# Attention on one core: TensorE's order laid over two key steps, every second values product cut into two halves of 256 queries

## Chip, cores and metric

One core of a Trainium2 chip (trn2) runs the kernel. The metric is the time of one execution on the device in microseconds (us); lower is better. Engines are named as in the profile: PE is TensorE (PEld its weight loads), DVE is VectorE, ACT is ScalarE, POOL is GpSimd and SP is SyncE, which issues the DMAs.

## What is computed

A transformer block with adaptive layer norm, on 2 sequences of 2048 tokens of 256 features, 16 heads of 16, all in 32-bit floats. Shortened:

```python
h = layernorm(x) * (1 + ca) + sa
q, k, v = split(h @ W_qkv.T + b_qkv)            # 16 heads of 16
logits = einsum('bhqd,bhkd->bhqk', q, k) / 4
logits = where(causal, logits, -inf)
o = einsum('bhqk,bhkd->bhqd', softmax(logits), v)
x = x + ga * (o @ W_out.T + b_out)
h = layernorm(x) * (1 + cb) + sb
x = x + gb * ffn(h)     # two linear maps, each with a routed low-rank part, relu between
```

The change touches only the attention in the middle.

## The kernel before

Three stages run one after the other: projections (to about 140 us of the profiled execution), attention (about 140 to 1005 us), output projection and feed-forward (to the end). Only the attention matters here.

**Tiling.** Heads go in 8 groups `g` of 4 (`GH`), queries in blocks `J` of 512. A pair (g, J) is a *unit*, 32 in all (line 39), with J running 0, 1, 2, 3 in one group and 3, 2, 1, 0 in the next. A unit has 4(J+1) *steps*, one for each 128 keys, so 4, 8, 12 or 16; all units together have 320 (`STEPS`, line 42). The last four steps of a unit lie on the causal diagonal: they skip 0, 128, 256 and 384 queries (`skip_of`) and add a mask. A unit's first step is always even and its last odd.

**A step n, by engine.** PE makes four logits tiles (line 811), one per head h: keys on the 128 partitions, up to 512 queries in the free dimension, into one of three PSUM banks (`L_BUFS` = 3, index 4n+h modulo 3). Even heads stand on rows 0 to 63 of the array, odd heads on rows 64 to 127. ACT takes the exponential of each tile into `prob` (line 1011). A logits tile must wait until the exponential three tiles earlier has freed its bank (line 809). Two steps later (`PV_LAG`) PE multiplies the values: `values(n - 2)` (line 829), four heads side by side in the array's column strips, 128 x 32 each, accumulated over the unit's steps in the one bank `O_BANK`. The weights `vw` hold values and ones, so the softmax denominator comes out too. `vw` and `prob` are plain 32-bit floats, and each product is recorded as two matmuls. At a unit's end ACT copies the bank out (`copy_out`, line 1002), and the next unit's first values wait for that (`o_out`, line 827).

**Fills.** The row maxima that the exponential needs are found one or more units ahead: PE makes queries-by-keys tiles, a *fill* (line 791), into two bank pairs (`S_BANK`), DVE reduces each (lines 1157 and 1161), and a fill waits until the fill two before it has been reduced (line 776). One fill is two matmuls of up to 512 columns, one on each half of the array's rows, and 4 or 8 mask matmuls more on the diagonal (line 767). Once per unit a *turn* fill (line 779) transposes the finished maxima, DVE copies them to `mT` (line 1186) and SP spreads them by four DMAs (line 470) into rows of the query stack; a unit's first logits wait for these (`m_in`, line 807).

**Order of the work.** PE's order is written out at lines 840 to 850. Which fills go into which step is planned by `slots()` (line 120): `ORDER[1 + n]` is the list for step n. There are 608 fills for 320 steps, 212 steps have two, 62 one, 29 three. Taken for each two steps (n even, n + 1), 86 of the 160 pairs have 4 fills, 24 have 2, 21 have 5, 16 have 3, the rest other numbers; of units 3 to 29, 19 pairs have 5 and 16 have 3. Units 30 and 31 have 3 fills in all.

**What the change and the steps of the prediction touch.** `mask` (762), `fill` (773), `logits` (800), `values` (820), PE's loop (840), and ACT's place for `copy_out` (1013).

Of the kernel before, what the change touches and what calls it, by code (L numbers as in the profile page):

```python
# [5 lines left out]
P = 128  # L6
# [17 lines left out]
BLK = 512  # L24
# [132 lines left out]
def until(eng, sem, count):  # L157
    if count > 0:
        eng.wait_ge(sem, count)


def build_program(nc, x, cT, wmod, wqkvT, bqkv, bv, woutT, bout, w1, b1, ar1, bl1, w2, b2, ar2, bl2, out):
# [4 lines left out]
    with ExitStack() as whole:  # L167
# [239 lines left out]
        with nc.Block() as block:  # L407
# [290 lines left out]
            def _(pe):  # L698
# [60 lines left out]
                    project(n)  # L759


                def mask(banks, col, table):

                    for half in range(2):
                        for par in range(2):
                            rows = slice(par * STACK, (par + 1) * STACK)
                            last = pe.matmul(ps[:, banks[par], col:col + P], eye_h[rows, half, :],  # L767
                                             table[rows, half, :], start=False, stop=True, skip_group_check=True)
                            if half == 1 and table is mask_kh:
                                last.then_inc(st_done, 1)  # L770
                    return last

                def fill(e):
                    ev = EVENTS[FILLS[e]]
                    bank = S_BANK + 2 * (e % 2)
                    until(pe, max_red, e - 1)
                    if ev[0] == "turn":
                        pe.wait_ge(m_low, ev[1] + 1)
                        pe.transpose(ps[:, bank, 0:P], mparts[:].bitcast(F32),
                                     ident[:]).then_inc(fill_done, 1)  # L780
                        return
                    _, u, r, pairs, cb, width, on_diagonal = ev
                    g, J = UNITS[u]
                    q, k = qst[g % 2], kst[g % 2]
                    if e == 0 or EVENTS[FILLS[e - 1]][0] == "turn" or EVENTS[FILLS[e - 1]][1] != u:
                        for j in range(J + 1):
                            pe.wait_ge(kq_in[g % 2][j], 16 * K_DMAS * (g // 2 + 1))
                    for at, p in enumerate(pairs):
                        for par in range(2):
                            rows = slice(par * STACK, par * STACK + ROWS)  # L790
                            last = pe.matmul(ps[:, bank + par, at * width:(at + 1) * width],  # L791
                                             q[rows, p, J * BLK + r * P:J * BLK + (r + 1) * P],
                                             k[rows, p, cb * BLK:cb * BLK + width],
                                             start=(at == 0), stop=True, skip_group_check=(at > 0))
                    if on_diagonal:
                        for at in range(len(pairs)):
                            last = mask((bank, bank + 1), (at + 1) * width - P, mask_qh)
                    last.then_inc(fill_done, 1)

                def logits(n, pair):  # L800

                    u, t = STEPS[n]
                    g, J = UNITS[u]
                    skip = skip_of(n)
                    banks = [L_BANK + (4 * n + 2 * pair + par) % L_BUFS for par in range(2)]
                    if n == FIRST[u] and pair == 0:
                        pe.wait_ge(m_in[u % 2], 16 * M_DMAS * (u // 2 + 1))
                    for par in range(2):
                        until(pe, exp_done, 4 * n + 2 * pair + par - L_BUFS + 1)
                        rows = slice(par * STACK, par * STACK + ROWS + MROWS)  # L810
                        last = pe.matmul(ps[:, banks[par], 0:BLK - skip],  # L811
                                         kst[g % 2][rows, pair, t * P:(t + 1) * P],
                                         qst[g % 2][rows, pair, J * BLK + skip:(J + 1) * BLK],
                                         start=True, stop=True)
                        if not diagonal(n):
                            last.then_inc(st_done, 1)
                    if diagonal(n):
                        mask(banks, 0, mask_kh)

                def values(n):  # L820
                    u, t = STEPS[n]
                    g, J = UNITS[u]
                    skip = skip_of(n)
                    pe.wait_ge(exp_done, 4 * (n + 1))
                    if n == FIRST[u]:
                        pe.wait_ge(v_wide, g + 1)
                        until(pe, o_out, u)
                    for h in range(GH):
                        last = pe.matmul(ps[32 * h:32 * h + 32, O_BANK, skip:BLK], vw[:, g % 2, t, h, :],  # L829
                                         prob[:, n % P_BUFS, h, 0:BLK - skip],  # L830
                                         start=(t == 0), stop=(n == LAST[u]), tile_position=(0, 32 * h))
                    last.then_inc(pv_done, 1)

                pe.wait_ge(h_out, NBLK * 2 * KC)
                pe.wait_ge(v_out, NBLK)
# [117 lines left out]
            def _(act):  # L953
# [45 lines left out]
                def copy_out(u):  # L999
                    act.wait_ge(pv_done, LAST[u] + 1)  # L1000
                    until(act, o_stored[u % 2], 16 * O_DMAS * (u // 2))
                    act.copy(o_sb[:, u % 2, :], ps[:, O_BANK, :]).then_inc(o_out, 1)  # L1002

                first_stage_over(act)
                for n in range(NS):
                    width = BLK - skip_of(n)
                    until(act, pv_done, n - P_BUFS + 1)
                    for h in range(GH):
                        i = 4 * n + h
                        act.wait_ge(st_done, i + 1)  # L1010
# [347 lines left out]
```

## Time and profile before

| | us |
|---|---|
| median of 3 runs | 1361.06 |
| lowest and highest of them | 1353.09, 1361.54 |
| the profiled execution, its own time | 1362.05 |
| its span, first to last instruction | 1360.2 |
| attention, first exponential to last step's | 139 to 1005 |
| granted TensorE clock, mean over the span | 0.948 of full |
| busy over the span: PE, DVE, ACT, POOL | 90%, 70%, 59%, 13% |

A busy share of PE is the time in which at least one matmul is recorded; the ends of matmuls are modelled, so the starts are the safer reading. An engine's idle time stands with what ended it.

### The profile page before, as it was taken

To read this page: it belongs to the slowest core of one execution; us is meant where nothing else is said; L and a number is where in the kernel's file an instruction comes from. 1 tells how busy PE (TensorE), PEld (TensorE's weight loads), DVE (VectorE), ACT (ScalarE), POOL (GpSimd) and SP (SyncE) were. 2 spreads that over 40 slices of the span, in tenths; PEclk is the share of its full clock that TensorE was granted. 3 is DMA by queue.
4 is the path that set the end of the run, shared out by engine and by line. 5 is a ranking of instruction groups with operands and counts; after the bars stand their busy time and mean duration, and the time that the engine had idled before them with its cause. 6 is when DMAs were issued, how large, how long until landed. Compare 5 with 4: busy or idle time off the path is not lost.

```text
span 1360.2 us, 23639 instructions
## 1 busy us (share of the span) xinstructions
PE 1221.2 (90%) x9456; PEld 714.0 (52%) x9456; DVE 950.9 (70%) x1247; ACT 804.3 (59%) x1616; POOL 175.7 (13%) x125
## 2 busy tenths in 40 slices
PE   2988889999999999999999999999962999999997
PEld 2875433444444444444444444434322888888886
DVE  7767897888787887787887777865203567666654
ACT  2542366777677777677777667777631544444442
POOL 8003700000111000000000000000003132323211
PEclk9987799999999999999999999999865999999999
DMA  4684130031041021031021021000013011111200
GB/s 154 217 267 175 40 72 10 8 84 35 31 115 47 10 77 37 10 89 40 9 62 52 10 79 49 9 9 11 9 34 123 1 62 49 42 43 55 63 16 32
DMA packets 58118, 79.53 MB, mean 58 GB/s; under 512 B 12680, under 2 KB 28752, under 8 KB 58008
## 3 DMA queue, kind: packets, MB, share of 16 engines
q1 hardware_dynamic: 58008, 78.01, 18.9%
q8 instruction: 75, 1.23, 0.4%
q14 instruction: 35, 0.29, 0.1%
HBM read 47.57 MB, written 29.62 MB: 57 GB/s over the span
## 4 chain that ended last, share of the span: by engine, by line
PE 66%; DVE 16%; ACT 8%; issue 7%; DMA 1%; POOL 1%; SPq 0%; POOLq 0%; ACTq 0%; DVEq 0%
PE ps L829 20%; PE ps L811 17%; PE ps L373 8%; PE ps L791 8%; ACT prob L1011 6%; PE ps L767 5%; PE ps L905 5%; DVE mx L1161 4%; DVE hid_lo L1273 4%; DVE xhat L401 2%; DVE stats L391 1%; ACT o_sb L1002 1%; DVE x L1227 1%; DVE x L1223 1%; DMA rd<-rden_rows 1%
## 5 line engine op out<-in xcount | busy, mean ns | idle before, releaser
L1011 ACT ACTIVATE prob<-ps 128x512 f32<-128x512 f32 (+3 forms) x1280 | 597.7, 535 | 258.1 <-PE ps L767 136.3
L1161 DVE TENSOR_REDUCE mx<-ps 128x2 f32<-128x1024 f32 (+1 forms) x512 | 593.2, 1190 | 171.7 <-PE ps L791 97.6
L811 PE MATMUL ps<-qst,kst 64*128 64x512 f32 (+3 forms) x1280 | 380.9, 448 | 13.1 <-ACT prob L1011 7.3
L811 PEld LDWEIGHTS ps<-qst,kst 64*128 64x128 f32 x1280 | 174.7, 186 | 323.7 <-ACT prob L1011 283.7
L829 PE MATMUL ps<-prob,vw 128*32 128x512 f32 (+3 forms) x2560 | 306.6, 551 | 9.8 <-ACT o_sb L1002 9.8
L791 PE MATMUL ps<-kst,qst 62*128 62x512 f32 (+3 forms) x1280 | 247.7, 417 | 20.9 <-DVE mx L1161 17.7
L791 PEld LDWEIGHTS ps<-kst,qst 62*128 62x128 f32 x1280 | 125.9, 191 | 64.0 <-DVE mx L1161 55.7
L767 PE MATMUL ps<-mask_kh,eye_h 64*128 64x128 bf16 x1024 | 100.6, 225 | 0.0
L829 PEld LDWEIGHTS ps<-prob,vw 128*32 128x32 f32 x2560 | 51.7, 108 | 74.6 <-ACT prob L1011 49.7
L1273 DVE TENSOR_TENSOR hid_lo<-hidf,hid_hi 128x512 fp32r<-128x512 f32 x64 | 73.1, 1182 | 12.8 <-ACT hid_hi L1055 12.7
L905 PE MATMUL ps<-w_hi,hid_hi 128*128 128x284 f32 x256 | 78.6, 328 | 2.0 <-ACT hid_hi L1055 2.0
L905 PE MATMUL ps<-w_lo,hid_hi 128*128 128x284 f32 x256 | 76.8, 321 | 0.0
L1157 DVE TENSOR_REDUCE mx<-ps 128x4 f32<-128x512 f32 x64 | 59.7, 954 | 21.6 <-PE ps L767 21.5
L1055 ACT ACTIVATE hidf<-ps,b_sb 128x512 f32<-128x512 f32 x64 | 44.0, 688 | 47.5 <-PE ps L894 47.5
L614 POOL COPY vw<-v_nat 128x1024 f32<-128x1024 f32 x8 | 8.3, 1040 | 469.0 <-PE ps L829 468.8
L767 PE MATMUL ps<-mask_qh,eye_h 64*128 64x128 bf16 x1024 | 66.6, 224 | 0.0
L373 PE MATMUL ps<-hT_hi,w_hi 128*128 128x512 f32 x128 | 53.2, 415 | 9.0 <-ACT hid_hi L1055 9.0
L905 PEld LDWEIGHTS ps<-w_hi,hid_hi 128*128 128x128 f32 x256 | 54.8, 214 | 4.0 <-ACT hid_hi L1055 3.6
L1038 ACT ACTIVATE gexp<-gexp 128x12 f32<-128x12 f32 x16 | 3.4, 212 | 89.4 <-DVE gexp L1243 89.4
L905 PEld LDWEIGHTS ps<-w_lo,hid_hi 128*128 128x128 f32 x256 | 55.0, 215 | 0.4
L667 POOL TENSOR_TENSOR o_raw<-o_raw,rd 128x1024 f32<-128x1024 f32 x8 | 19.5, 2440 | 254.2 <-DMA rd<-rden_rows 254.2
L767 PEld LDWEIGHTS ps<-mask_kh,eye_h 64*128 64x128 bf16 x1024 | 42.9, 97 | 17.1 <-issue 7.2
(150 smaller groups left out, 1402.8 us busy)
## 6 DMA issues: line engine op xcount, KB each, us to landing
qk_parts<-parts SPq DMA_DIRECT2D x32, 512.0 KB, 4.2
qst<-qk_parts SPq DMA_DIRECT2D x192, 64.0 KB, 2.3
kst<-qk_parts SPq DMA_DIRECT2D x192, 64.0 KB, 2.3
xs<-in_x SPq DMA_DIRECT2D x16, 512.0 KB, 7.2
o_all<-o_sb SPq DMA_DIRECT2D x32, 256.0 KB
o_raw<-o_all SPq DMA_DIRECT2D x16, 256.0 KB
rd<-rden_rows SPq DMA_DIRECT2D x16, 256.0 KB
out<-y SPq DMA_DIRECT2D x8, 512.0 KB, 3.1
```

The costliest lines, as they stand in the source:

```text
L373: last = pe.matmul(out, lhs(i, k), rhs(j, k), start=(start and k == 0 and n == 0), stop=(stop and k == chunks - 1 and n == len(PASSES) - 1))
L401: last = dve.tensor_scalar(xhat[:, t, :], xs[:, t, :], mv[:, t, 0:1], rstd[:, t:t + 1], ALU.subtract, ALU.mult)
L767: last = pe.matmul(ps[:, banks[par], col:col + P], eye_h[rows, half, :], table[rows, half, :], start=False, stop=True, skip_group_check=True)
L791: last = pe.matmul(ps[:, bank + par, at * width:(at + 1) * width], q[rows, p, J * BLK + r * P:J * BLK + (r + 1) * P], k[rows, p, cb * BLK: ...
L811: last = pe.matmul(ps[:, banks[par], 0:BLK - skip], kst[g % 2][rows, pair, t * P:(t + 1) * P], qst[g % 2][rows, pair, J * BLK + skip:(J + ...
L829: last = pe.matmul(ps[32 * h:32 * h + 32, O_BANK, skip:BLK], vw[:, g % 2, t, h, :], prob[:, n % P_BUFS, h, 0:BLK - skip], start=(t == 0), ...
L905: last = pe.matmul(ps[:, Y_BANK + t, 0:D + ZP], hid[u][:, m, t * P:(t + 1) * P], w2_p[v][:, m, :], start=(e == 0), stop=(e == len(order) - 1))
L1011: act.activation(prob[:, n % P_BUFS, h, 0:width], ps[:, L_BANK + i % L_BUFS, 0:width], ACT.Exp).then_inc(exp_done, 1)
L1055: act.activation(dst, ps[:, H_BANK + m % 2, :], ACT.Relu, bias=b1_sb[:, m:m + 1]).then_inc(f1_out, 1)
L1157: dve.tensor_reduce(mx[:, u % 2, :, :, r, cb], ps[:, bank:bank + 2, 0:2 * width].rearrange("p a (h x) -> p a h x", h=2), AX, ALU.max).then ...
L1161: dve.tensor_reduce(mx[:, u % 2, :, pairs[0], r, cb], ps[:, bank:bank + 2, 0:width], AX, ALU.max).then_inc(max_red, 1)
L1273: dve.tensor_tensor(hid[1][:, m, :], hidf[:, m % HRING, :], hid[0][:, m, :].bitcast(F32), ALU.subtract).then_inc(hid_lo_done, 1)
```

## The change

PE's order is laid over two steps, n even and n + 1. The logits of single heads, or of pairs that are not of the same step, alternate with fills and with the values of step n - 2, cut into two halves of the queries; the values of step n - 1 stay whole. `logits` takes a list of heads. The key mask is added right behind each such list, for its heads. The first three fills of the two steps have fixed places, all the others go to the end. ACT's copy of a finished unit comes one step later than before, less one head. Lags, buffers, the planner and all other engines' orders stay. Core of the diff:

```diff
-                def logits(n, pair):
+                def logits(*heads):
+                    for n, h in heads:
...
+                        until(pe, exp_done, 4 * n + h - L_BUFS + 1)
...
+                    if diagonal(heads[0][0]):
+                        mask_keys(heads)
...
-                def values(n):
+                def values(n, part=None):
...
+                    lo, hi = 0, BLK - skip
+                    if part == 0:
+                        hi = hi // 2
+                    if part == 1:
+                        lo = hi // 2
                     pe.wait_ge(exp_done, 4 * (n + 1))
-                    if n == FIRST[u]:
+                    if n == FIRST[u] and part != 1:
                         pe.wait_ge(v_wide, g + 1)
                         until(pe, o_out, u)
...
-                for n in range(NS):
+                for n in range(0, NS, 2):
+                    es = [*ORDER[1 + n], *ORDER[2 + n]]
+                    logits((n, 0), (n, 1))
+                    for e in es[0:1]:
+                        fill(e)
+                    logits((n, 2))
                     if n >= PV_LAG:
-                        values(n - PV_LAG)
-                    logits(n, 0)
-                    for e in ORDER[1 + n][:2]:
+                        values(n - 2, 0)
+                    logits((n, 3), (n + 1, 0))
+                    for e in es[1:2]:
                         fill(e)
-                    logits(n, 1)
-                    for e in ORDER[1 + n][2:]:
+                    if n >= PV_LAG:
+                        values(n - 2, 1)
+                    logits((n + 1, 1))
+                    for e in es[2:3]:
                         fill(e)
-                for n in range(NS - PV_LAG, NS):
-                    values(n)
+                    logits((n + 1, 2), (n + 1, 3))
+                    if n >= PV_LAG:
+                        values(n - 1)
+                    for e in es[3:]:
+                        fill(e)
+                values(NS - 2)
+                values(NS - 1)
...
-                        if h == 1 and n - PV_LAG in UNIT_AT_END:
-                            copy_out(UNIT_AT_END[n - PV_LAG])
+                        if h == 0 and n - PV_LAG - 1 in UNIT_AT_END:
+                            copy_out(UNIT_AT_END[n - PV_LAG - 1])
```

`mask_keys(heads)` adds, for each half of the key mask, one matmul per head of the list, and raises `st_done` with the second.

## Rows read from the trace of the kernel before

**Rows 1.** The page: busy time, share, instructions; the clock in 40 slices.

```profile
PE 1221.2 (90%) x9456; PEld 714.0 (52%) x9456; DVE 950.9 (70%) x1247; ACT 804.3 (59%) x1616; POOL 175.7 (13%) x125
...
PEclk9987799999999999999999999999865999999999
```

**Rows 2.** Busy time by window (us; instructions; clock, DMA share, GB/s), one unit each.

```profile
645.70:687.70 42.00, 41.09 (x325) 17.03 (x321) 34.87 (x35) 31.52 (x66) 0.00 (x0) 1.00 0.02 8
594.00:614.38 20.38, 19.50 (x160) 8.30 (x156) 16.81 (x16) 14.83 (x34) 0.00 (x0) 1.00 0.36 98
614.38:645.70 31.32, 29.88 (x257) 13.00 (x253) 23.09 (x25) 23.25 (x50) 0.00 (x0) 1.00 0.14 40
584.16:594.00 9.84, 9.38 (x97) 4.96 (x93) 7.88 (x11) 6.51 (x18) 1.04 (x1) 1.00 0.27 88
...
971.15:1006.00 34.85, 31.29 (x211) 11.80 (x203) 3.27 (x6) 20.94 (x48) 0.00 (x0) 0.76 0.05 17
```

**Rows 3.** Timeline of one step: start, duration, engine, line [idle before <- releaser].

```profile
599.68 0.50 PE L811 MATMUL ps<-qst,kst 64*128 64x512 f32 x2
600.02 0.40 PE L791 MATMUL ps<-kst,qst 62*128 62x512 f32 x2
600.25 0.40 PE L791 MATMUL ps<-kst,qst 62*128 62x512 f32 x2
600.27 2.07 ACT L1011 ACTIVATE prob<-ps 128x512 f32<-128x512 f32 x4 [0.74 <-PE ps L811]
600.48 0.40 PE L811 MATMUL ps<-qst,kst 64*128 64x512 f32 x1
600.92 0.18 PEld L811 LDWEIGHTS ps<-qst,kst 64*128 64x128 f32 x1 [0.48 <-ACT prob L1011]
601.35 1.07 PE L829 MATMUL ps<-prob,vw 128*32 128x512 f32 x8
602.35 0.50 PE L811 MATMUL ps<-qst,kst 64*128 64x512 f32 x2
602.94 2.07 ACT L1011 ACTIVATE prob<-ps 128x512 f32<-128x512 f32 x4 [0.60 <-PE ps L811]
```

**Rows 4.** Waits, 227 to 950 us: who for whom, total, times, longest.

```profile
PEld ps L811 <- ACT prob L1011: 249.3, 396, 0.9
...
PEld ps L791 <- DVE mx L1161: 29.3, 75, 0.8
```

**Rows 5.** Groups by form, 300 to 900 us: count, busy us, mean ns, idle before.

```profile
L1161 DVE TENSOR_REDUCE mx<-ps 128x2 f32<-128x1024 f32 x319 | 380.2, 1221 | 91.5 <-PE ps L791 68.1 <-PE ps L767 20.1
L1011 ACT ACTIVATE prob<-ps 128x512 f32<-128x512 f32 x630 | 331.1, 601 | 101.9 <-PE ps L811 78.9 <-PE ps L767 22.0
```

**Rows 6.** Chain of work on the diagonal: start us, us, what.

```profile
678.56 0.13 PE ps L767 x4
...
682.70 0.33 PE ps L767 x3
...
685.51 0.78 PE ps L829 x8
...
687.55 0.57 PE ps L829 x8
```

**Rows 7.** Timeline where a unit begins.

```profile
647.73 0.42 PE L829 MATMUL ps<-prob,vw 128*32 128x128 f32 x8
648.08 0.69 PE L811 MATMUL ps<-qst,kst 64*128 64x512 f32 x2
...
649.65 0.59 ACT L1002 COPY o_sb<-ps 128x512 f32<-128x512 f32 x1
...
650.39 1.06 PE L829 MATMUL ps<-prob,vw 128*32 128x512 f32 x8 [0.41 <-ACT o_sb L1002]
```

**Rows 8.** Timeline of a unit's maxima on SP.

```profile
220.74 2.60 SPq L470 DMA_DIRECT2D qst<-mT  x4
```

**Rows 9.** Timeline where the clock is low.

```profile
768.16 1.93 PE L829 MATMUL ps<-prob,vw 128*32 128x512 f32 x8
...
770.02 0.29 PEld L811 LDWEIGHTS ps<-qst,kst 64*128 64x128 f32 x2 [1.66 <-issue]
```

More of the change, by code:

```diff
@@ L759, in _, with mask_queries @@
                     project(n)
-                def mask(banks, col, table):
+                def mask_queries(bank, col):
                     for half in range(2):
@@ L766, in mask, with mask_keys @@
                             rows = slice(par * STACK, (par + 1) * STACK)
-                            last = pe.matmul(ps[:, banks[par], col:col + P], eye_h[rows, half, :],
-                                             table[rows, half, :], start=False, stop=True, skip_group_check=True)
-                            if half == 1 and table is mask_kh:
+                            last = pe.matmul(ps[:, bank + par, col:col + P], eye_h[rows, half, :],
+                                             mask_qh[rows, half, :], start=False, stop=True, skip_group_check=True)
+                    return last
+                def mask_keys(heads):
+                    for half in range(2):
+                        for n, h in heads:
+                            rows = slice(h % 2 * STACK, (h % 2 + 1) * STACK)
+                            last = pe.matmul(ps[:, L_BANK + (4 * n + h) % L_BUFS, 0:P], eye_h[rows, half, :],
+                                             mask_kh[rows, half, :], start=False, stop=True, skip_group_check=True)
+                            if half == 1:
                                 last.then_inc(st_done, 1)
-                    return last
                 def fill(e):
@@ L796, in fill @@
                         for at in range(len(pairs)):
-                            last = mask((bank, bank + 1), (at + 1) * width - P, mask_qh)
+                            last = mask_queries(bank, (at + 1) * width - P)
                     last.then_inc(fill_done, 1)
-                def logits(n, pair):
+                def logits(*heads):
+                    for n, h in heads:
+                        u, t = STEPS[n]
+                        g, J = UNITS[u]
+                        skip = skip_of(n)
+                        if n == FIRST[u] and h == 0:
+                            pe.wait_ge(m_in[u % 2], 16 * M_DMAS * (u // 2 + 1))
+                        until(pe, exp_done, 4 * n + h - L_BUFS + 1)
+                        rows = slice(h % 2 * STACK, h % 2 * STACK + ROWS + MROWS)
+                        last = pe.matmul(ps[:, L_BANK + (4 * n + h) % L_BUFS, 0:BLK - skip],
+                                         kst[g % 2][rows, h // 2, t * P:(t + 1) * P],
+                                         qst[g % 2][rows, h // 2, J * BLK + skip:(J + 1) * BLK],
+                                         start=True, stop=True)
+                        if not diagonal(n):
+                            last.then_inc(st_done, 1)
+                    if diagonal(heads[0][0]):
+                        mask_keys(heads)
+                def values(n, part=None):
                     u, t = STEPS[n]
@@ L804, in logits @@
                     skip = skip_of(n)
[L805 to L818, printed above, removed]
-                def values(n):
-                    u, t = STEPS[n]
-                    g, J = UNITS[u]
-                    skip = skip_of(n)
+                    lo, hi = 0, BLK - skip
[3 more added lines that the diff above has]
+                        lo = hi // 2
                     pe.wait_ge(exp_done, 4 * (n + 1))
-                    if n == FIRST[u]:
+                    if n == FIRST[u] and part != 1:
                         pe.wait_ge(v_wide, g + 1)
@@ L828, in values @@
                     for h in range(GH):
[L829 to L832, printed above, removed]
+                        last = pe.matmul(ps[32 * h:32 * h + 32, O_BANK, skip + lo:skip + hi], vw[:, g % 2, t, h, :],
+                                         prob[:, n % P_BUFS, h, lo:hi],
+                                         start=(t == 0 and part != 1), stop=(n == LAST[u] and part != 0),
+                                         tile_position=(0, 32 * h), skip_group_check=True)
+                    if part != 0:
+                        last.then_inc(pv_done, 1)
                 pe.wait_ge(h_out, NBLK * 2 * KC)
```

## Prediction

> **What bounds the kernel now.** I read the page first: PE is recorded busy for 90% of the span, DVE for 70% and ACT for 59% [rows 1]. That looks like a PE-bound kernel, in which an order can bring nothing. The windows by unit say the same (41.09 of 42.00 us on PE, 34.87 on DVE, 31.52 on ACT [rows 2]), but a recorded matmul includes its latency, so I went to the starts in the timeline of one step [rows 3].
>
> The step is a loop with a fixed length. Call the four logits tiles L0 to L3 and their exponentials E0 to E3. L0 and L1 start at 599.68; E0 starts at 600.27, 0.59 later; L3 needs the bank that E0 frees and its weights load at 600.92, 0.65 later; the values start at 601.35 (0.43) and the next L0 at 602.35 (1.00). Sum 0.59 + 0.65 + 0.43 + 1.00 = 2.67 us, and nearly all full steps of units 3 to 29 take that, with one fill or two. ACT works 2.07 of it and idles 0.60. So neither engine is full: the wait of L3 for E0 sets the pace. The table of waits confirms it: PE's loads of logits weights waited 249.3 us for the exponential, 396 times, against 29.3 us for DVE [rows 4].
>
> From the same rows come PE's true costs. The first slot behind a values visit takes 0.34 (599.68 to 600.02, its weight load in the open), each further slot 0.23 (600.02, 600.25, 600.48). A slot is up to two matmuls, one per half of the rows. A single tile loaded in the open and followed by values takes 0.43, so with its weights already loaded about 0.43 - 0.11 = 0.32. A values visit of 512 columns takes 1.00. With two fills PE's own work in a step is 0.34 + 0.23 + 0.23 + 0.32 + 1.00 = 2.12; the other 0.55 is the wait.
>
> **The change, a full pair of steps with 4 fills.** Before: 2 x 2.67 = 5.34. After, with F0 to F3 the fills, t = 0 at F3, which follows the whole values, and L0 to L7 the eight tiles:
> - F3 0, L0 and L1 0.34, F0 0.57, L2 0.80, half values at 1.12. For a half I take the visit of 256 columns, 0.57 [rows 6]; two halves cost 1.14 against 1.00.
> - L3 at 1.69. L4 needs E1. E0 starts 0.49 behind L0's loaded start (0.40 of matmul and 0.09 to ACT), at 0.83; exponentials follow each other by (2.07 - 0.60) / 3 = 0.49 [rows 3, 5], so E1 starts at 1.32 and ends at 1.92, L4 loads at 1.97: a wait of 0.28. F1 at 2.31 (0.11 load, 0.23), half values at 2.63, to 3.20.
> - L5 with F2's even half 0.34, F2's odd half with L6 0.23, L7 0.32, whole values at 4.09, next F3 at 5.09. E2 (1.81), E3 (2.30) and E4 (2.79, done 3.4) are in time for L5, L6 and L7.
>
> So 5.09, of which 4.81 is PE's work (0.57 more than before) and 0.28 a wait (1.10 before). Gain 0.25 per full pair. ACT needs 8 x 0.49 = 3.9. DVE starts reductions every 1.14 us (two in 2.36, one takes 1.22 [rows 5]), so four need 4.56: covered, but close. Without F3 the pair takes 0.34 less, since before the loop hid that fill for nothing.
>
> **The other pairs.**
> - Unit's first pair: its values are narrow (256 columns in two halves at 0.35 each, then 128, 0.35 from 647.73 to 648.08 [rows 7]). With the same timetable and no F3 left from the pair before: about 4.0.
> - Second pair: the copy of the finished unit now stands behind E0, so it starts at 0.83 + 0.49 = 1.32, takes 0.59, and the values start some 0.14 behind it (650.39 against 650.24 [rows 7]), at 2.05 instead of 1.12. L4's wait is swallowed; period about 5.7.
> - Diagonal pairs: masks cost 0.13 behind a pair and up to 0.33 at the end of a group [rows 6]; five groups now, four before, and single heads no longer share a slot with a fill. Adding up gives 10.1 for the last two pairs against about 10.0. No gain there.
>
> Units of 16 steps: 4.0 + 5.7 + 4 x 5.09 + 10.1 = 40.2 against 42.00; of 12: 4.0 + 5.7 + 10.2 + 10.1 = 30.0 against 31.32 (I take -1.4); of 8: 19.8 against 20.38; of 4: about 9.7 against 9.84 [rows 2]. Units 3 to 29 are 8, 7, 6 and 6 of these: 8 x 1.8 + 7 x 1.4 + 6 x 0.6 + 6 x 0.15 = 28.7 us.
>
> **Where it gives back.** 19 pairs there have 5 fills, and two of them now stand together at the end. The next pair's F0 needs the first one's bank: matmul 0.49, reduction 1.22, hand-overs 0.09 make 1.80, while PE is there after 0.34 + 0.23 + 0.23 = 0.80. That holds PE for 1.0 us, less the 0.28 of L4, plus a slot of 0.23: 0.95. What is queued behind F0 is L2, and behind it the values. Before, three fills in a step cost some 0.3 themselves. Net +0.6 each, +11.4. The 16 pairs with 3 fills save 0.34 each, -5.4.
>
> Turn fills of units 1 to 3 move to the end of the next to last pair, two steps before the logits that wait for them instead of three or more. Their four DMAs take 2.60 us to issue [rows 8] and land later still; the last pair covers some 4.3. I take +2 in all (0 to 6). The units before 3 carry three fills a step and are paced by DVE: no change. Units 30 and 31 run partly at clock 0.76 [rows 2] and have few fills: -1 (+4 to -6, as the clock falls).
>
> Cut values raise PE's instructions, not the wait counts of other engines; `prob` has four buffers, and ACT never comes near that wait. POOL's and SP's later work for a unit moves by one step and has several steps of room.
>
> **Sum.** -28.7 + 11.4 - 5.4 + 2 - 1 = -21.7. The profiled execution took 1362.05, 1.0 above the median; 1362.05 - 21.7 = 1340.3, so I say 1340.
>
> **A rule weighed.** The rows show that going from logits to values and back costs 0.14 more than the streaming of a 256-column visit's two passes (0.57 against 0.43) plus 0.11 for a load in the open. The Trainium skill, TensorEngine Tiling (Array Packing), Key Properties, says that changing the tiling mode, not just the tile, drains TensorE; logits are row tiles and values column tiles, so the new order has six such changes in two steps instead of four. By that rule alone the change would cost and not save; the trace agrees that each has a price, and that price is in the 4.81 above.
>
> **Rivals.**
> - *The switches eat the gain.* If a half costs 0.70 rather than 0.57, or single tiles don't share slots with the fills next to them (up to three slots of 0.23 where I counted them shared), a full pair is at 5.3 to 5.4 and nothing is left: 1356 to 1366, say 1361. For it: no lone tile next to a fill is in the rows with both weights loaded. Against: the 0.57 is measured on the same instruction form. Chance 0.20.
> - *More falls away.* L4 waits less (E0 follows a loaded pair by 0.43 if ACT's hand-over is short), and the end fills don't hold PE, because DVE has its slack when they come. -28.7 - 5.4 and another 100 x 0.06: about 1322. Chance 0.18.
> - *The clock falls (slower).* At half clock a whole values visit takes 1.86 (768.16 to 770.02 [rows 9]) instead of 1.00. Place: the first two pairs of a unit, where streams are narrow and PE now waits 0.9 us for the copy. Before, it happened once in units 3 to 29 (the visit of rows 9) and again at the end. It decides from 11 such falls on; one in each of 31 units adds about 60 and gives 1400, half as many 1370. Against: elsewhere PE idles less than before. Chance 0.12, typical time 1380.
>
> **How the numbers follow.** Forecast 0.50, rivals 0.20, 0.18, 0.12. The forecast's own spread is 1330 to 1351. A difference under 1% (13.6 us) is what a measurement here can't tell from none. Faster by over 1% (below 1347.5): 0.44 of the forecast's 0.50 and the 0.18, 0.62. Slower by over 1% (above 1374.7): 0.11, most of the clock rival. The rest, 0.27, is same. Range 1318 to 1362: low from the second rival with its bounds, high from the middle of the first; 0.2 stays outside, the clock rival and the edges of the others.
>
> **What would show it.** Right: full pairs start every 5.1 us; the longest wait on PE is L4's, 0.3 us once in two steps, so logits waiting for exponentials fall from 249 us to under 80; ACT's busy share rises slightly; line 829's visits number 480 for 320 steps; values behind a copy wait about 0.9 us. The DVE waits of the fills rise above 29 us. Wrong: full pairs at 5.3, halves above 0.6, lone tiles that start only after the fill beside them, or more slices of the clock under 9 between 230 and 950 us.

## The result: slightly slower, and the profile after

| | before | after |
|---|---|---|
| median, us | 1360.21 (4 runs, 1353.09 to 1361.54) | 1372.59 (4 runs, 1364.18 to 1377.42) |
| ratio, 95% interval | | 1.0084 (1.0048 to 1.012) |
| the profiled execution, span | 1360.2 | 1368.1 |

The kernel became 0.8% slower. That is inside the 1% I called "same", with its interval (0.5 to 1.2%) wholly on the slow side; I had forecast 1340 us and a range up to 1362.

The page of the kernel after first: busy time and the clock by slices. Beside [rows 1], PE has 1272 matmuls and 11 us of busy time more, DVE 6 and ACT 4 us; the shares are the same.

```profile
PE 1232.6 (90%) x10728; PEld 747.3 (55%) x10728; DVE 956.7 (70%) x1247; ACT 808.5 (59%) x1616; POOL 175.6 (13%) x125
...
PEclk9998599999999999999999999999985899999998
```

Where the time went shows when the attention is cut just ahead of unit 3 and unit 28, at the start of the last exponential of the unit before. The last window ends at the last exponential of the step before the last; the first begins with the load of ACT's table at 139.2, which the rows before counted as the first exponential (that one starts at 140.5). Columns after the window: its length, busy us (instructions) of PE, PEld, DVE, ACT and POOL, granted clock, DMA share, GB/s. After:

```profile
139.20:234.34 95.14, 82.71 (x689) 39.71 (x691) 76.92 (x79) 46.10 (x98) 22.23 (x14) 0.80 0.15 40
234.34:919.69 685.35, 660.68 (x6747) 318.41 (x6743) 535.96 (x567) 492.91 (x1050) 24.15 (x38) 1.00 0.15 43
919.69:1014.84 95.15, 92.70 (x936) 43.59 (x932) 41.89 (x48) 74.92 (x162) 0.00 (x0) 1.00 0.03 11
827.75:847.53 19.78, 19.38 (x192) 8.81 (x188) 17.40 (x16) 14.88 (x34) 0.00 (x0) 1.00 0.37 98
664.12:706.64 42.52, 41.31 (x389) 18.82 (x385) 34.79 (x34) 31.58 (x67) 0.00 (x0) 1.00 0.02 8
```

The same cuts before:

```profile
139.24:227.20 87.96, 74.45 (x609) 34.64 (x611) 75.12 (x79) 45.73 (x99) 22.32 (x14) 0.90 0.18 44
227.20:898.13 670.93, 649.65 (x5723) 290.60 (x5719) 532.97 (x568) 488.51 (x1050) 24.18 (x38) 1.00 0.15 44
898.13:1004.62 106.49, 98.19 (x773) 40.60 (x769) 41.66 (x49) 75.18 (x161) 0.00 (x0) 0.93 0.03 12
```

So +7.2 us in units 0 to 2, +14.4 in units 3 to 27, -11.3 in units 28 to 31, and -2.3 behind the attention. Unit 25 (8 steps, the fourth window) takes 19.78 against 20.38 for a unit of its kind, unit 19 (16 steps) 42.52 against 42.00 [rows 2].

**The plain pair came out as worked out.** The timeline of PE in the third pair of unit 11, four fills and none on the diagonal:

```profile
459.54 0.50 PE L799 MATMUL ps<-kst,qst 62*128 62x512 f32 x2
459.88 0.39 PE L818 MATMUL ps<-qst,kst 64*128 64x512 f32 x2
460.12 0.39 PE L799 MATMUL ps<-kst,qst 62*128 62x512 f32 x2
460.35 0.39 PE L818 MATMUL ps<-qst,kst 64*128 64x512 f32 x1
460.66 0.64 PE L843 MATMUL ps<-prob,vw 128*32 128x256 f32 x8
461.23 0.78 PE L818 MATMUL ps<-qst,kst 64*128 64x512 f32 x2
461.57 0.67 PE L799 MATMUL ps<-kst,qst 62*128 62x512 f32 x2
462.18 0.64 PE L843 MATMUL ps<-prob,vw 128*32 128x256 f32 x8
462.75 0.49 PE L818 MATMUL ps<-qst,kst 64*128 64x512 f32 x1
462.75 0.72 PE L799 MATMUL ps<-kst,qst 62*128 62x512 f32 x2
463.08 0.62 PE L818 MATMUL ps<-qst,kst 64*128 64x512 f32 x2
463.63 1.06 PE L843 MATMUL ps<-prob,vw 128*32 128x512 f32 x8
464.62 0.51 PE L799 MATMUL ps<-kst,qst 62*128 62x512 f32 x2
```

From the first start, half values come 1.12 later, L3 at 1.69, half values at 2.64, L5 beside the fill's even half at 3.21, whole values at 4.09, the next F3 at 5.08. The prediction had 1.12, 1.69, 2.63, 3.20, 4.09, 5.09. L4's wait is the 0.78 of two matmuls at 461.23.

**What the other pairs do.** Because the load of the table was counted as an exponential, every boundary of a pair, here and in the experiments, is one exponential early: a pair's time runs from the last exponential before it to its own last one. Sums over units hardly change by that, but the split between neighbouring pairs does. The last column has the split between true first exponentials. After - before in us, in all, units 3 to 27:

```
kind of pair                                 pairs   as counted   first exponentials
follows a pair with five or more fills          19      +18.8          +18.3
has five or more fills, follows none such       16       -8.0           -3.3
of the rest: has fills on the diagonal          40      +10.3          +12.9
of the rest: no fill on the diagonal            53       -6.8          -13.5
```

### The profile page after: what moved, and what is told of

It reads as the page before. It is cut to its first block, busy times and chain, and to the rows that moved or that the text cites. A ratio compares the mean times of both kernels' runs of the same rounds, so it can differ in the third digit from the quotient of the medians.

```text
span 1368.1 us, 26183 instructions
## 1 busy us (share of the span) xinstructions
PE 1232.6 (90%) x10728; PEld 747.3 (55%) x10728; DVE 956.7 (70%) x1247; ACT 808.5 (59%) x1616; POOL 175.6 (13%) x125
## 4 chain that ended last, share of the span: by engine, by line
PE 72%; DVE 18%; ACT 4%; issue 3%; DMA 1%; SPq 0%; POOL 0%; DVEq 0%; ACTq 0%; POOLq 0%
PE ps L843 21%; PE ps L818 18%; PE ps L799 10%; PE ps L373 9%; PE ps L933 7%; DVE mx L1189 5%; DVE hid_lo L1301 4%; PE ps L776 3%; DVE xhat L401 2%; PE ps L767 2%; ACT prob L1039 2%; ACT o_sb L1030 1%; DVE stats L391 1%; DVE x L1255 1%; DVE x L1251 1%
## 5 line engine op out<-in xcount | busy, mean ns | idle before, releaser
L818 PE MATMUL ps<-qst,kst 64*128 64x512 f32 (+3 forms) x1280 | 389.8, 434 | 0.6 <-ACT prob L1039 0.4
L843 PE MATMUL ps<-prob,vw 128*32 128x256 f32 (+1 forms) x3832 | 340.5, 428 | 12.7 <-ACT o_sb L1030 12.5
L799 PE MATMUL ps<-kst,qst 62*128 62x512 f32 (+3 forms) x1280 | 320.7, 433 | 28.6 <-DVE mx L1189 25.7
L818 PEld LDWEIGHTS ps<-qst,kst 64*128 64x128 f32 x1280 | 186.0, 188 | 177.8 <-ACT prob L1039 138.0
L799 PEld LDWEIGHTS ps<-kst,qst 62*128 62x128 f32 x1280 | 147.4, 192 | 124.9 <-DVE mx L1189 60.7
L843 PEld LDWEIGHTS ps<-prob,vw 128*32 128x32 f32 x3832 | 77.2, 109 | 126.9 <-issue 61.9
L776 PE MATMUL ps<-mask_kh,eye_h 64*128 64x128 bf16 x1024 | 106.5, 225 | 0.0
L767 PE MATMUL ps<-mask_qh,eye_h 64*128 64x128 bf16 x1024 | 79.3, 225 | 0.0
L373 PE MATMUL ps<-hT_hi,w_lo 128*128 128x512 f32 x128 | 50.9, 398 | 0.0
```

The costliest lines, as they stand in the source:

```text
L373: last = pe.matmul(out, lhs(i, k), rhs(j, k), start=(start and k == 0 and n == 0), stop=(stop and k == chunks - 1 and n == len(PASSES) - 1))
L767: last = pe.matmul(ps[:, bank + par, col:col + P], eye_h[rows, half, :], mask_qh[rows, half, :], start=False, stop=True, skip_group_check= ...
L776: last = pe.matmul(ps[:, L_BANK + (4 * n + h) % L_BUFS, 0:P], eye_h[rows, half, :], mask_kh[rows, half, :], start=False, stop=True, skip_g ...
L818: last = pe.matmul(ps[:, L_BANK + (4 * n + h) % L_BUFS, 0:BLK - skip], kst[g % 2][rows, h // 2, t * P:(t + 1) * P], qst[g % 2][rows, h // ...
L843: last = pe.matmul(ps[32 * h:32 * h + 32, O_BANK, skip + lo:skip + hi], vw[:, g % 2, t, h, :], prob[:, n % P_BUFS, h, lo:hi], start=(t == ...
```

## Experiments

All times below are medians with the kernel before of the same chips beside them, and ratios to it. The kernel after was not timed again with them; its ratio is 1.0084.

### Where the fifth fill stands

**e1_spread.** The kernel after, with a pair's fills dealt out differently.

```diff
-                    for e in es[3:]:
+                    for e in at[3]:      # at = places(es): one maxima fill per place,
                         fill(e)          # a turn fill goes in front of the next one
```

> Kernel after, with the fifth fill of a pair of steps moved: a turn fill goes in front of the fill that follows it and takes no place of its own, so each of the four places has one maxima fill (lists of more than four maxima fills are divided as evenly as they go). No fill stands behind another one at the end of a pair. Theory, the held bank: in the kernel after, a pair that follows one with five fills is about 1.0 to 1.4 us longer (5.77 us for the last pair of a unit of 16 steps against 4.49 us where the pair before had four), since the first of two fills at the end has not been reduced when the next pair's first fill wants its bank. Then these pairs fall to 4.5 us (last of a unit) and some 0.9 us each are won, 19 times: -14 to -20 us in units 3 to 27, and some us in units 0 to 2, which would put it at 1343 to 1358, with the kernel after at about 1370 and before at 1360. Rival, these pairs are long by their own masks and narrow tiles: they stay at 5.7 us and the time stays within 4 us of the kernel after.

Measured 1369.87 against 1360.1, ratio 1.0058 (1.0022 to 1.0094): 0.3 points under the kernel after, with intervals that overlap, so no gain to speak of. Pair by pair, both sides of the expectation hold. The last pair of unit 11 falls from 5.78 to 4.48 us, as the held bank says, and the pair with the turn rises from 5.49 to 6.52. The reason is one line of its trace: the fill behind the turn now finds the bank of the fill before the turn unreduced.

```profile
477.49 0.51 PE L799 MATMUL ps<-kst,qst 62*128 62x512 f32 x2 [0.71 <-DVE mx L1197]
```

A turn uses a bank pair like any fill. Put next to another fill anywhere, it makes two in a row; the hold only moved one pair ahead. Part of the rest is the clock, which was at half for 24 us of units 3 to 31 here (10 in the profiled execution after).

**e10_fourth_fill_before_values.** The kernel after, with two of the fills moved apart.

```diff
+                    end = 4 if len(es) >= 5 else 3
+                    for e in es[3:end]:
+                        fill(e)
                     if n >= PV_LAG:
                         values(n - 1)
-                    for e in es[3:]:
+                    for e in es[end:]:
```

> Kernel after; in pairs with five or more fills the fourth stands before the whole values instead of behind them, so the last two are a values visit (1.00 us) apart. Theory, the held bank: the first of the two is reduced 1 us earlier, the next pair's first fill waits 0.2 us instead of 1.0, and the pair after one with a turn and four fills falls from 5.77 us (last pair of a unit) to 4.7 to 4.9, while the pair with five fills stays at 5.5 to 5.7. 19 times 0.6 to 0.9 us: -11 to -17 us against the kernel after, 1353 to 1361. Rival, DVE has no slack in these pairs and the time only moves, as it did where the turn shared the first place (5.5 to 6.5 us there, 5.77 to 4.48 behind it): within 5 us of the kernel after.

Measured 1358.0 against 1359.96, ratio 0.9988 (0.9966 to 1.001), so 1.0% or 13 us less than the kernel after. The hold in the kernel after, in the last pair of unit 11 (486.54 is the first of the two fills at the end, 487.09 its reduction, and the next pair's first fill stands until that is over):

```profile
484.00 2.58 DVE L1189 TENSOR_REDUCE mx<-ps 128x2 f32<-128x1024 f32 x2 [1.16 <-PE ps L799]
...
486.54 0.74 PE L799 MATMUL ps<-kst,qst 62*128 62x512 f32 x4
...
487.09 2.36 DVE L1189 TENSOR_REDUCE mx<-ps 128x2 f32<-128x1024 f32 x2 [0.51 <-PE ps L799]
...
488.37 0.19 PEld L799 LDWEIGHTS ps<-kst,qst 62*128 62x128 f32 x2 [1.01 <-DVE mx L1189]
```

DVE had been idle for 1.16 and 0.51 us shortly before: it had the time, not the data. In e10 the same place reads:

```profile
477.60 1.07 PE L843 MATMUL ps<-prob,vw 128*32 128x512 f32 x8
478.59 0.49 PE L799 MATMUL ps<-kst,qst 62*128 62x512 f32 x2
...
479.53 0.50 PE L799 MATMUL ps<-kst,qst 62*128 62x512 f32 x2 [0.19 <-DVE mx L1192]
```

The last pair is 5.17 instead of 5.78, the one with five fills unchanged at 5.49. In the traces, units 3 to 27 take 10 us less than in the kernel after and units 0 to 2, where the edit acts too, 3 us less. Of all that the new order costs this is the largest part that one edit took away.

### Masked fills: work that the old wait covered

**e2_after_mask_work_twice, e3_before_mask_work_twice.** Both kernels, with the query mask's matmuls of each diagonal fill issued again with a table of zeros.

```diff
+                            for half in range(2):
+                                for par in range(2):
+                                    ...
+                                    last = pe.matmul(ps[:, bank + par, col:col + P], eye_h[rows, half, :],
+                                                     none_h[rows, half, :], start=False, stop=True, ...)
```

> Kernel after, with the query mask's matmuls of every diagonal fill issued a second time against a table of zeros (same result; 512 more places of two 128-column matmuls side by side, 400 of them in units 3 to 27). It doubles the work whose price in the new order I had left out. Theory, exposed PE work: without the long wait for the exponential nothing covers it, so each place costs its 0.06 us except where a pair still waits: +20 to +30 us against the kernel after. Rival, pairs with diagonal fills are slow in the kernel after for another reason (the reductions, or the bank pairs): under +10 us.

> Kernel before, with the same doubled query mask matmuls. Theory: in the old order a step's third logits wait 0.45 us for the first exponential behind the fills, so the doubled work fits into that wait for the most part: +2 to +10 us against the kernel before, and at least 12 us less than the same edit costs in the kernel after. Rival, it is no matter of cover: both orders pay the same, 20 us or more.

Measured: after with doubled masks 1398.8, ratio 1.0249 (1.0189 to 1.0309), so +1.65 points or 22 us over the kernel after, as expected. Before with doubled masks 1377.31, ratio 1.0113 (1.0083 to 1.0143), +15 us, more than the 2 to 10 expected, and the gap between the two only 7 us instead of at least 12.

The pairs tell why. Unit 11 has three pairs in a row whose 12 fills include its six on the diagonal, all in the first two pairs (16 places of two mask matmuls side by side); without masks they would take three plain pairs:

```
                                     three pairs, us    beyond plain pairs
before                               16.00              0.0  (3 x 5.34)
before, masks doubled                16.51             +0.5
after                                16.25             +1.0  (3 x 5.09)
after, masks doubled                 17.02             +1.8
```

In the old order the first helping of masks costs nothing and the second half a microsecond: the cover, L3's wait [rows 3, 4], was for the most part used up by the masks that were there. My expectation for e3 took it for free. A step of the kernel before with two diagonal fills, eight mask matmuls, starts its next logits after 2.67 us like one without [rows 3]:

```profile
460.78 0.50 PE L811 MATMUL ps<-qst,kst 64*128 64x512 f32 x2
...
461.35 0.29 PE L767 MATMUL ps<-mask_qh,eye_h 64*128 64x128 bf16 x4
...
461.76 0.29 PE L767 MATMUL ps<-mask_qh,eye_h 64*128 64x128 bf16 x4
...
463.45 0.50 PE L811 MATMUL ps<-qst,kst 64*128 64x512 f32 x2
```

In the new order the first helping costs 0.06 us a place at once. The timeline after, with masks between fill and logits, each of them on PE's path (0.21 us for the four places from 470.30, 0.10 for the two from 471.00):

```profile
469.95 0.50 PE L799 MATMUL ps<-kst,qst 62*128 62x256 f32 x4
470.30 0.40 PE L767 MATMUL ps<-mask_qh,eye_h 64*128 64x128 bf16 x8
470.51 0.48 PE L818 MATMUL ps<-qst,kst 64*128 64x512 f32 x2
470.82 0.33 PE L799 MATMUL ps<-kst,qst 62*128 62x384 f32 x2
471.00 0.29 PE L767 MATMUL ps<-mask_qh,eye_h 64*128 64x128 bf16 x4
471.10 0.48 PE L818 MATMUL ps<-qst,kst 64*128 64x512 f32 x1
```

Other units say the same. Take the pairs with four fills inside a unit, off the diagonal and not behind five fills, between first exponentials: before, all 18 take 5.33 or 5.34 us; after, the seven without masks take 5.08, the eight with 8 places 5.58, and the two with 12 places also 5.58. Units 3 to 27 have 400 such places, so I estimate at most 400 x 0.06 = 24 us for what the prediction left out. The masks were not taken away in a run, only doubled, so the price of the first helping rests on these comparisons of pairs and starts.

### The cut and the change of tiling

**e4_before_cut_in_place.** The kernel before, with every even step's values in two halves that stay together.

```diff
+                    cuts = (0, width // 2, width) if n % 2 == 0 else (0, width)
+                    for c, (lo, hi) in enumerate(zip(cuts, cuts[1:])):
                         for h in range(GH):
```

> Kernel before, with the values of every even step cut into two halves of the queries that stay next to each other. It prices the cut alone, without a change of tiling between the halves. In the old order the values lie on the loop that sets the step. If two halves cost 0.57 each against 1.00 (0.14 more), 160 cuts give +22 us. If the extra of a visit is only its way in and out (the halves follow each other without draining), it is 0.03 each, +4 us. Rival: a cut costs more than I took, 0.3 us, +48 us.

Measured 1361.4 against 1360.1, ratio 1.0003 (0.9976 to 1.0031). A cut whose halves stay together costs nothing that shows. The interval excludes +22 us and reaches +4, so the time alone leaves my lower figure of 0.03 us a cut open; the starts speak against it. A visit with 16 matmuls of 256 columns ends where one with 8 of 512 does, 1.00 us later:

```profile
657.36 1.07 PE L832 MATMUL ps<-prob,vw 128*32 128x256 f32 x16
658.36 0.50 PE L811 MATMUL ps<-qst,kst 64*128 64x512 f32 x2
```

So the 0.14 that two separate halves cost over a whole (0.57 twice against 1.00) is the way in and out, between values and logits. The Trainium skill, TensorEngine Tiling (Array Packing), Key Properties, says that a change of the tiling mode drains TensorE; this run agrees, in that the price follows the change and not the cut.

**e7_whole_values.** The kernel after, with the cut undone.

```diff
-                        values(n - 2, 0)
+                        values(n - 2)
...
-                    if n >= PV_LAG:
-                        values(n - 2, 1)
```

> Kernel after, with the values of the even step whole in the place of their first half. It undoes the cut and nothing else. By my timetable a pair with four fills off the diagonal then takes 5.28 us (PE stands at the sixth and seventh logits for the exponentials of the fourth and fifth), against 5.09 us with halves and 5.34 us in the old order. Two changes of tiling fewer save 0.35 us of PE's work in each pair, so pairs with masked fills, where PE's work decides, get shorter by up to 0.3 us. In all within 8 us of the kernel after. Rival, the switches are what costs the kernel after its gain: then every pair gets shorter and it is 15 us or more faster than the kernel after.

Measured 1373.76, ratio 1.0107 (1.0079 to 1.0135), within 0.3 points of the kernel after. The plain pair takes 5.23 us in its timeline, where 5.28 was worked out:

```profile
459.23 0.50 PE L799 MATMUL ps<-kst,qst 62*128 62x512 f32 x2
...
462.56 0.98 PE L818 MATMUL ps<-qst,kst 64*128 64x512 f32 x2
463.46 1.06 PE L843 MATMUL ps<-prob,vw 128*32 128x512 f32 x8
464.46 0.50 PE L799 MATMUL ps<-kst,qst 62*128 62x512 f32 x2
```

The 0.98 of two matmuls at 462.56 is the wait of L7. The cut is worth 0.15 us a plain pair, and it is not what made the kernel slower. That refutes the rival of the switches, by which every pair had to get shorter. The pairs with masks did not gain their 0.3 us either: the two of unit 11 take 10.86 us together, and 10.78 in the kernel after.

### The two ends of the attention

**e6_old_first_units.** The kernel after, with units 0 to 2 in the old order: `if not NEW[n]:` runs the old loop's body for the two steps, and ACT's copy goes where that needs it.

> Kernel after, with units 0 to 2 in the old order. In the kernel after these units take 95.2 us against 88.0 us, and the clock is at half for 39 us of them against 17 us; the list of the first pair has 14 fills, of which 11 stand in one row at its end, where PE issues a fill each 1.14 us and does nothing else. Theory, the bunch of fills lets the clock stay low and delays the first units: -5 to -8 us against the kernel after. Rival, the clock's stretches there are chance: within 3 us.

Measured 1362.28 against 1361.05, ratio 1.0016 (0.9997 to 1.0035): 9 us less than the kernel after. The first three units take 90.9 us in this trace, and 95.1, 98.4, 92.1 and 90.9 in the traces of the new order that keep the bunch (after, e2, e10, e7), against 88.0, 90.0, 88.9, 88.0 and 90.8 in those of the old (before, e3, e4, e5, e8). In e1, which has the new order but deals these fills out, they take 87.7 us, with 19 us at half clock: one trace, but it points to the bunch and not to the rest of the new order. That the bunch of 11 fills does this by way of the clock is not settled: the half clock in this stretch was 39 us after, 39 in e2, but 25 in e7, and 28 here in the old order. The part it costs is 4 us by the traces and 9 by the medians; the path was not isolated.

**e5_late_only.** The old order up to unit 26, the new one from unit 27 on.

> Old order (kernel before) up to unit 26, new order from the first pair of unit 27 on, with ACT's copy of a unit placed to match. Theory: the new order pays where a pair has at most three fills and few of them on the diagonal, since then PE's work for a pair is short and the wait for the exponential is what goes. The two traces give -1.7 us for unit 27 and -10.4 us for units 28 to 31 (the sum of the pairs' differences), so 1346 to 1352 with before at 1360. Rival: the late part is faster in the kernel after only because its clock happened to be high there (its low stretches between 940 and 1014 us are absent, before has 10 us of them): then no more than -5 us.

Measured 1347.42 against 1361.05, ratio 0.991 (0.9883 to 0.9937). Units 28 to 31 take 92.1 us up to the last pair, in this trace as in that of the kernel after, and 91.1 to 95.6 in the eight others with the new order there; the three traces with the old order (before, e3, e4) have 102.5 to 103.1. In those three the clock fell in unit 30, in the two pairs with one fill each (8.30 and 6.66 us before, instead of 5.5 and 5.7); in no trace of the new order did it fall there, though in two (e2, e10) it was at half for 3.4 us in unit 28. So I estimate that some 4 of the 10 us come from the clock that stays up and 6 from shorter pairs.

**e8_mixed, e9_mixed_turned, e11_turned_old_order.** Each kind of pair in the order that is shorter for it; the same with the old order turned, so that logits come first and values last in each step; the turned old order alone.

```diff
+                        for m in (n, n + 1):
+                            logits((m, 0), (m, 1))
+                            for e in ORDER[1 + m][:2]:
+                                fill(e)
+                            logits((m, 2), (m, 3))
+                            for e in ORDER[1 + m][2:]:
+                                fill(e)
+                            if m >= PV_LAG:
+                                values(m - 2)
```

> Each pair of steps in the order that was shorter for its kind in the two traces: the new order for pairs of units 3 to 27 with at most four fills, none of them on the diagonal (the second pair of a unit also with them), which do not follow a pair with five fills and are not the last of a unit, and for units 28 to 31; the old order for all others. 67 pairs and the last units are in the new order. The sum of the pairs' measured differences is -20 us, if each keeps its time beside neighbours of the other kind: 1340 us with before at 1360. If gains are given back at the seams, or the clock falls more often, half of that: 1350.

Measured 1347.95, ratio 0.9907 (0.9888 to 0.9926). The edit puts 48 pairs of units 3 to 27 and the 20 of the last four units in the new order. Units 3 to 27 gained nothing (672.8 us against 670.9): in unit 12 an old pair behind a new one took 7.02 instead of 5.17 us, and the new one behind it 4.38 instead of a plain 5.09, a loss of 1.1 at that seam.

> The same choice of pairs as in the mixed kernel, but the old order is turned in its circle: a step's two pairs of logits and its fills first, the values of two steps ago last, so that every pair of steps, old or new, begins with logits and ends with values. ACT's copy of a unit has the place of the new order everywhere. Theory, the mixed kernel lost its gain at the seams (whole values, the end fill, and whole values again stand in a row where an old pair follows a new one, 7.02 us for a pair of 5.15 us, and the next new pair gets back 0.7 of it): without them the sum of the pairs' differences comes, -17 to -22 us against before: 1339 to 1344. Rival, new pairs need new neighbours (their gain comes from the phase of the exponentials that the pair before leaves): no better than the mixed kernel, 1348.

Measured 1351.48, ratio 0.9941 (0.9919 to 0.9964): wrong. The seam is smaller, not gone (6.53 and 5.04, where 5.17 and 5.47 stand in the pure kernels): the rival is right that a new pair's gain needs new neighbours.

> All pairs in the turned old order of the kernel just described; the control for it. The circle of logits, fills and values is the same as in the kernel before, entered at another place, so full steps take 2.67 us and the time is that of the kernel before within 4 us, the beginnings of units apart, where the copy of the finished unit comes later. If it were 5 us or more faster, the turn and not the new order would be what helps.

Measured 1349.42 against 1359.96, ratio 0.9933 (0.9907 to 0.9959). I had expected a difference within 4 us. In the traces 7 us of the gain lie in units 3 to 27 and 5 in units 28 to 31. Steps inside a unit are the same (5.34 a pair), but the second pair of unit 11 takes 4.75 instead of 5.49 us, for 0.13 and 0.22 lost in the first and the last; between first exponentials it is the first pair that falls, from 5.33 to 4.35, and 0.15 and 0.42 are lost. A unit's first values no longer wait 0.41 us for the copy [rows 7]: such waits came to 9.8 us in 25 visits between 227 and 1000 us before, and the turned order's trace lists none. PE makes the logits first, and the copy lies beside them. PE's and ACT's timelines there, with no wait in front of the values:

```profile
441.58 0.61 ACT L1044 COPY o_sb<-ps 128x512 f32<-128x512 f32 x1
...
441.95 0.40 PE L821 MATMUL ps<-qst,kst 64*128 64x512 f32 x2
442.33 1.07 PE L846 MATMUL ps<-prob,vw 128*32 128x512 f32 x8
443.32 0.50 PE L821 MATMUL ps<-qst,kst 64*128 64x512 f32 x2
```

**e12_turned_then_new.** The turned old order up to unit 26, the new one from unit 27 on: `NEW = {n: n >= FIRST[27] for n in range(0, NS, 2)}`.

> The turned old order up to unit 26, the new order from unit 27 on. It joins the two parts that were found shorter: the turned order wins some 7 us in units 3 to 26 over the kernel before (the copy of a finished unit no longer holds the values of the next), and units 28 to 31 take 92.1 us in the new order against 97.3 in the turned and 102.5 in the old one. If the two add up: 1360 - 7 - 10 - 2 = 1341, ratio 0.984 to 0.989, faster than either alone (0.991 for the late part alone, 0.993 for the turned order alone). Rival, the two win the same thing (the copy's wait at the units' beginnings): no better than 0.990.

Measured 1341.62 against 1360.35, ratio 0.9851 (0.9826 to 0.9877): the two gains add, and this beats both kernels. Its windows for the same three parts (units 0 to 2, 3 to 27, 28 to 31):

```profile
139.40:228.94 89.54, 75.77 (x601) 34.97 (x603) 75.04 (x79) 45.75 (x99) 22.24 (x14) 0.87 0.17 43
228.94:893.50 664.56, 648.28 (x5787) 292.96 (x5783) 532.93 (x568) 489.99 (x1051) 24.12 (x38) 1.00 0.17 44
893.50:988.40 94.90, 92.45 (x936) 43.46 (x932) 41.92 (x48) 74.90 (x162) 0.00 (x0) 1.00 0.03 11
```

## Why the prediction was wrong

**What held.** The reading of the bound held: not a full engine but L3's wait for E0. Loads of logits that wait for an exponential fell from 249.3 us [rows 4] to 110.7 in the same window; I had said under 80. Every start of the plain pair was met within 0.01 us, e7's pair within 0.05, unit 25 came out at 19.78 where 19.8 was worked out, and the hold behind five fills at 1.01 us where 1.0 was. The first two pairs of unit 11 take 4.25 and 5.73 us between first exponentials, where 4.0 and 5.7 were worked out. The waits after, 227 to 950 us; the last is that of the values for the copy, which I had at about 0.9 each:

```profile
PEld ps L818 <- ACT prob L1039: 110.7, 290, 0.8
...
PEld ps L799 <- DVE mx L1189: 35.6, 59, 1.3
...
PE ps L843 <- ACT o_sb L1030: 10.6, 23, 0.8
```

**What failed**, by the parts of the sum. For units 3 to 27 it comes to -17 us (-25.5 for the pairs, +11.4 for the fifth fills, -3.1 for the 9 pairs there with three); measured +14.4, so 31.6 too low. (One subtraction was off: units of 12 steps give 1.3 and not 1.4, 0.7 us in all.)

- *Steady pairs all costed as plain.* The step "4 x 5.09" for a unit of 16 steps took the timetable without mask matmuls for every pair inside a unit. A third of the maxima fills lie on the diagonal, and in the planner's lists they stand in pairs of all kinds, not only in the diagonal steps. I had priced the key mask and left out the query mask. Diagonal fills cost 1.0 us in three pairs of unit 11, by estimate at most 24 us over the stretch, and the 40 pairs that have them are at +12.9 between first exponentials where the prediction's terms for their places (first pair -1.3, second +0.4, inside -0.25, diagonal 0) come to some -4. This is the largest failure, about 17 us. The cause in one sentence: the wait that the change removed had been covering work, and of that cover I priced the fill and not its masks. How much of the 17 us is masks and how much other things in the same pairs was not separated.
- *The fifth fill, mis-sized.* Forecast +0.6 for each. The 35 pairs that have five fills or follow such a pair came out at +15.0 (+10.8 as counted), where their places alone would give some -4: that is 1.0 for each of the 19 (0.8), so 3 to 8 us too little. Where the pair behind is a unit's last, as in six cases, the hold shows nearly whole: 5.28 us in unit 11 against 4.23 in e1, between first exponentials, and no wait of L4 swallows 0.28 of it, as I had assumed for all.
- *The rest of the pairs.* Some 7 us more, spread, and not followed further.
- *The first units, costed at nothing.* +7.2 against +2. DVE was taken to set the pace there whatever the order. e6 wins 9 us, by what path is open.
- *The last units, too low.* -11.3 against -6.6: the clock stayed up, which I had given no gain.

Added up, with -2.3 behind the attention: -21.7 + 31.6 + 5.2 - 4.7 - 2.3 = +8.1, against +7.9 between the two spans.

**Rivals.** The switches were counted rightly (e4, e7). In units 3 to 31 the clock was at half for less time than before, 10 us against 22; the executions of the kernel after spread over 13 us, those of before over 8. A time like the measured one I had reached only by the clock rival, with its chance of 0.12, and it came for another reason: no rival of mine had work that comes out from under a wait.

## What to carry to other kernels

Before a wait is taken off the critical path, list everything that runs while it lasts, by every form of it and not by the commonest, since each becomes path when the wait goes; the form that is a third of all cases decided here. Two producers behind each other into a double buffer hold the third, however idle the consumer is, so spread them by the consumer's time. And try the same circle of work entered at another point: it left the steps inside a unit as they were and took the wait for the copy at a unit's boundary off the path.

## What the runs showed of the hardware

- Cutting a column-tiled product of 512 columns into two of 256 that stay together costs nothing (1.00 us either way, e4); separated by logits, the two take 0.57 each (460.66 to 461.23 and 462.18 to 462.75 in the kernel after).
- Single logits do share the array with the half of a fill on the other rows: L5 and a fill's even half both start at 462.75 in the kernel after.
- The granted clock fell without a long idle stretch of PE. With the old order it went from full to half in unit 30 for 10.2 us in three traces of three, at 975.6 us in the kernel before, behind 20 us in which PE was recorded busy for 17.84 and stood still for half a microsecond at most. In the kernel after PE is recorded busy through all of the same stretch, and with the new order the clock stayed at full there in every trace. The turned old order (e11) had 18.14 of 20 us and kept full clock, e3 had 18.03 and fell, so these traces do not say what decides. Columns as before; before, then after:

```profile
955.60:975.60 20.00, 17.84 (x171) 8.03 (x165) 5.50 (x10) 14.71 (x34) 0.00 (x0) 1.00 0.01 2
...
970.69:990.69 20.00, 20.00 (x227) 9.72 (x223) 7.53 (x11) 15.42 (x35) 0.00 (x0) 1.00 0.01 2
```
